# Four buffers for layer 0's normalised rows, and a fourth stage in the expert tiles of a two-layer kernel

## What is computed

```python
    x = L0_attn_u
    xn = _layernorm(x, axis=-1)
    x = x + _L0_attn_ref(xn, ...) + _L0_ffn_ref(xn, ...)
    xn = _layernorm(x, axis=-1)
    x = x + _L1_attn_ref(xn, ...) + _L1_ffn_ref(xn, ...)
```

## Time and profile before

| what | value |
|---|---|
| median of three runs | 1592.26 us |
| the profiled execution's own time | 1595.26 us |
| its span, first to last instruction | 1593.5 us |
| PE busy | 1453.8 us (91%) |
| DVE, ACT, POOL busy | 839.1, 526.5, 578.4 us |
| mean granted TensorE clock | 0.954 of full |
| chain that ended last | PE 86%, DVE 5%, issue 4%, DMA 2%, ACT 1% |

### The profile page before, as it was taken

How to read it: one execution, slowest core, us unless ns; L and a number is a source line. 1 busy time by engine, 2 the same in 40 slices (tenths; PEclk the granted TensorE clock), 3 DMA queues, 4 the chain that set the end, 5 groups by cost and what they waited for, 6 DMA issues and landing times.

```text
span 1593.5 us, 29535 instructions
## 1 busy us (share of the span) xinstructions
PE 1453.8 (91%) x10753; PEld 1151.7 (72%) x10753; DVE 839.1 (53%) x2307; ACT 526.5 (33%) x1099; POOL 578.4 (36%) x762
## 2 busy tenths in 40 slices
PE   7996999999999998999997899999998979997866
PEld 6886789999999997666665566666665647776744
DVE  4554444444444443788875666666666534333414
ACT  2221122222222222333332545454444434433300
POOL 2444421111111111222224455646563454455460
PEclk9998999999999999999997999999999989999987
DMA  5893811111111114100002111111100004434431
GB/s 177 149 104 44 99 48 50 52 47 48 48 50 51 47 48 122 38 0 0 0 0 64 31 31 32 28 34 27 36 21 15 2 18 129 134 119 133 120 123 62
DMA packets 73185, 94.77 MB, mean 59 GB/s; under 512 B 14877, under 2 KB 61367, under 8 KB 73056
## 3 DMA queue, kind: packets, MB, share of 16 engines
q1 hardware_dynamic: 55440, 56.54, 15.6%
q0 software_dynamic: 17616, 36.48, 8.3%
HBM read 60.66 MB, written 32.31 MB: 58 GB/s over the span
## 4 chain that ended last, share of the span: by engine, by line
PE 86%; DVE 5%; issue 4%; DMA 2%; ACT 1%; another core or an unknown queue 1%; POOL 0%; DVEq 0%; ACTq 0%; POOLq 0%
PE score L1591 49%; PE mixed L1591 18%; PE side L1591 13%; DVE WGU L1458 2%; PE side L1793 2%; DMA xn_rows<-XN 2%; PE side L1600 1%; PE mixed L1960 1%; PE side L1953 1%; PE side L1739 0%; PE side L1858 0%; DVE stats L1027 0%; DVE X L1483 0%; DVE X L1558 0%
## 5 line engine op out<-in xcount | busy, mean ns | idle before, releaser
L707 POOL DMA_INDIRECT XN<-xn_rows,slot_tok x149 | 141.4, 949 | 399.5 <-PE side L1793 365.3
L1458 DVE TENSOR_REDUCE WGU<-score 128x2 f32<-128x256 f32 (+1 forms) x256 | 130.8, 553 | 153.3 <-PE score L1591 151.2
L1591 PE MATMUL score<-xT,HT 128*128 128x128 f32 x1136 | 208.0, 275 | 0.0
L743 POOL TENSOR_SCALAR_AFFINE_SELECT ARENA<-ARENA 128x256 f32<-128x256 f32 x256 | 104.2, 431 | 185.1 <-ACT ARENA L944 184.0
L1591 PEld LDWEIGHTS score<-xT,HT 128*128 128x128 f32 x1136 | 166.8, 192 | 0.0
L944 ACT ACTIVATE ARENA<-score 128x768 f32<-128x768 f32 x128 | 103.8, 811 | 148.3 <-PE score L1591 145.9
L1257 DVE TENSOR_TENSOR HT<-sh_gu,score 128x128 f32<-128x128 f32 (+1 forms) x149 | 71.3, 478 | 148.7 <-ACT sh_gu L909 71.3
L657 POOL DMA_INDIRECT lists<-token_no,w_in x128 | 125.4, 980 | 44.2 <-issue 32.3
L1591 PE MATMUL score<-ARENA 32*128 32x256 f32 (+1 forms) x2048 | 126.8, 353 | 12.0 <-DVE WGU L1458 6.0
L1591 PE MATMUL mixed<-ARENA,HT 128*128 x568 | 134.2, 379 | 0.0
L909 ACT ACTIVATE sh_gu<-score 128x128 f32<-128x128 f32 (+1 forms) x149 | 64.1, 430 | 191.3 <-PE score L1591 172.8
(11 more groups left out here) (249 smaller groups left out, 2714.8 us busy)
## 6 DMA issues: line engine op xcount, KB each, us to landing
y_rows<-sh_gu SPq DMA_DIRECT2D x149, 128.0 KB
xn_rows<-XN SPq DMA_DIRECT2D x32, 256.0 KB
WGU<-in_gu SPq DMA_DIRECT2D x8, 1024.0 KB
X<-in_u SPq DMA_DIRECT2D x16, 256.0 KB
ARENA<-in_dn SPq DMA_DIRECT2D x8, 512.0 KB
out<-X SPq DMA_DIRECT2D x16, 256.0 KB
XN<-xn_rows,slot_tok POOLq DMA_INDIRECT x149
lists<-token_no,w_in POOLq DMA_INDIRECT x128
```

The source lines that it names most:

```text
L707: x["got"][j % RING].mark(eng.indirect_dma_start(XG[j % RING], None, xn_rows[l], bass.IndirectOffsetOnAxis(slot_tok[:, j:j + 1], 0)))
L743: ins = eng.affine_select(out=m, in_=m, compare_op=ALU.is_ge, fill=0.0, base=0, pattern=[[0, 2], [1, P]], channel_multiplier=-1)
L1458: ins = eng.tensor_reduce(o, score[:, 2 * h:2 * h + 2, c * P:(2 * c + 1) * P], AX.X, ALU.max, negate=True)
L1591: return eng.matmul(o, l, r, start=start, stop=stop)
```

## The change

Three things are done.

The normalised rows of layer 0 get four buffers, `XN0`: the two of `XN` and two in the region of `ARENA` that later holds the last expert's down weights. Sequence n uses buffer n % 4, and `norm_apply` waits for the store of sequence n-4. The wait for PE's transposes of sequence n-2 stays. The load of the last expert's down weights waits for the last transposes and for the last stores from the two new buffers.

The expert tiles of both layers get a stage `ahead` between `new` and `r`. Tile t is gathered, transposed and copied in turn t, its weights are copied in turn t+1 (`ahead`), its gate and up products come in turn t+2, its down product in turn t+3. There is one turn more. On PE `down` now comes ahead of `xt`, and on ACT `y_copy` ahead of `xt_copy`.

`UPS` has seven sequences in place of eight, seven turns apart from turn 46 on rather than six; nine come after the tiles. `finals` moves the early `finish` calls two turns back.

The diff, cut to its core (the other places pass the buffers on: the waits ahead of layer 0's gathers on POOL, and the operands of the transposes):

```diff
@@ -34,7 +34,7 @@
-UPS = {20: 0, 40: 1, 46: 2, 52: 3, 58: 4, 64: 5, 70: 6, 76: 7}
+UPS = {20: 0, 40: 1, 46: 2, 53: 3, 60: 4, 67: 5, 74: 6}
@@ -144,18 +144,19 @@
-    return [[tile(t - k, count) for k in range(3)] for t in range(count + 2)]
+    return [[tile(t - k, count) for k in range(4)] for t in range(count + 3)]
...
-    end = N1 + 2
+    end = N1 + 3
+    finals = {FINALS_AT + 5 + 4 * n: n for n in range(EARLY)}
     for t in range(end + NSEQ - EARLY + 2):
...
-        last = (t - FINALS_AT - 3) // 4 if t < end and (t - FINALS_AT - 3) % 4 == 0 else EARLY + t - end - 2 if t > end + 1 else None
-        yield t, [tile(t - k) for k in range(3)], *(None if n is None else of(n) for n in (up, down, last))
+        last = finals.get(t) if t < end else EARLY + t - end - 2 if t > end + 1 else None
+        yield t, [tile(t - k) for k in range(4)], *(None if n is None else of(n) for n in (up, down, last))
@@ -260,6 +261,8 @@
     XN = [sb(f"XN{u}", [P, CH, D]) for u in range(2)]
+    last_dn = ARENA[:, (E - 1) * I0 // P * D:].rearrange("p (u c d) -> p u c d", u=2, c=CH)
+    XN0 = [t[:, :, :] for t in XN] + [last_dn[:, u, :, :] for u in range(2)]
@@ -381,7 +384,7 @@
-        n["stored"] = [ev(f"norm_stored{u}", 1, 16, "sync", b // 2) for u in range(2)]
+        n["stored"] = [ev(f"norm_stored{u}", 1, 16, "sync", b // len(XN0)) for u in range(len(XN0) if l == 0 else 2)]
@@ -551,10 +554,15 @@
             N[0]["xn"].wait(eng, n)
-            N[0]["stored"][n % 2].mark(eng.dma_start(rows0[:, n * CH:(n + 1) * CH, :], XN[n % 2][:, :, :]))
+            v = n % len(XN0)
+            N[0]["stored"][v].mark(eng.dma_start(rows0[:, n * CH:(n + 1) * CH, :], XN0[v]))
...
         for e in range(E):
+            if e == E - 1:
+                N[0]["tr"].wait(eng, NSEQ - 1)
+                for v in (2, 3):
+                    N[0]["stored"][v].wait(eng, NSEQ // len(XN0) - 1)
@@ -913,13 +921,13 @@
-            def body(new, r, old):
+            def body(new, ahead, r, old):
                 if r:
                     silu(r)
+                if old:
+                    y_copy(old)
                 if new:
                     xt_copy(new)
-                if old:
-                    y_copy(old)
@@ -1036,10 +1044,15 @@
-            ne["stored"][r.u].wait(eng, r.half, 1)
+            if l == 0:
+                rows, turn = XN0[r.n % len(XN0)], r.n // len(XN0)
+                ne["stored"][r.n % len(XN0)].wait(eng, turn, 1)
+            else:
+                rows = XN[r.u]
+                ne["stored"][r.u].wait(eng, r.half, 1)
@@ -1256,15 +1269,15 @@
-            def body(new, r, old):
-                if new and l == 1:
-                    both_weights(new)
-                if new and l == 0 and new.n:
-                    gate_weights(new)
+            def body(new, ahead, r, old):
+                if ahead and l == 1:
+                    both_weights(ahead)
+                if ahead and l == 0 and ahead.n:
+                    gate_weights(ahead)
                 if r:
                     h_stage(r)
-                if new and l == 0 and new.n:
-                    up_weights(new)
+                if ahead and l == 0 and ahead.n:
+                    up_weights(ahead)
@@ -1823,15 +1837,15 @@
-            def body(new, r, old):
+            def body(new, ahead, r, old):
                 if r:
                     gate(r)
                     if l == 0:
                         up(r)
+                if old:
+                    down(old)
                 if new:
                     xt(new)
-                if old:
-                    down(old)
```

9 lines of the change are left out of this document (5 added, 4 removed).

## The result

The changed kernel takes 1581.45 us, median of four runs (1577.64 to 1582.5), against 1592.12 for the kernel before on the same occasion (1591.78 to 1592.51): ratio 0.9929, interval 0.9911 to 0.9946. It is 10.7 us faster. I had forecast 22.8 us less and 1569.5 us, so the sign was right, the size less than half, and the time inside the range (1556 to 1584) near its slow end.

What follows compares the result with a forecast made beforehand. PE bounds layer 0's tiles, with slack at the front, in layer 1's tiles and behind them. Terms -8.0 - 13.0 - 7.0 + 5.2 = -22.8 us give 1572.5, less 3.0 for the median: 1569.5 us, range 1556 to 1584.

Steps and rivals of the forecast that it cites:

- Four row buffers: Front: DVE's and PE's waits for a late store of normalised rows go, less some given back; -8.0 us.
- I take back 2.7 us: Front: part of the 10.7 us gain returned, about a quarter of ACT's 9.86 us wait after eight scatters.
- Layer 0's tiles: The extra stage there gains nothing, since PE has no idle time and does the same products reordered; 0 us.
- Turns 1 to 46: Layer 1's tiles: PE's wait for ACT's copy goes, 42 turns save 0.31 us each; -13.0 us.
- From turn 46: Layer 1's later tiles: one shared sequence leaves (5.2 us) and 1.8 us of PE's waits go; -7.0 us.
- Behind the tiles: After the last tile: the ninth shared sequence comes on top; +5.2 us, with ends 0 and +9.
- Rival 1: Second half of layer 1's tiles: POOL's unseen stops double, +5.6 there, 1582 us in all; 14 in 100.
- Rival 2: Second half of layer 1's tiles: PE never holds POOL up again, -19 there, 1557.5 us; 15 in 100.
- Rival 3: Front gives nothing, because the scatters' landing sets the lists and the gain is waited for again; 1577.5 us; 10 in 100.
- Rival 4: Layer 1's tiles: POOL's DMAs stretch by one 0.44 us weight copy per turn; 1589.4 us; 3 in 100.
- Rival 5: ACT's 30.6 us stop comes inside layer 1's tiles, with PE behind it; 1600 us; 5 in 100.
- standstill: Behind the tiles: ACT stands still 30.59 us while POOL issues 32 indirect DMAs; used as fact, cause unknown.

Runs made afterwards that it cites:

- paced_burst: Changed kernel with POOL's last 32 gathers in groups of four, each waiting until the previous sequence is added: 1562.36 us, ratio 0.9793 to the kernel before.
- front_only: Kernel before with nothing but the four row buffers: 1589.63 us, ratio 0.9975 to the kernel before.
- after_again: Changed kernel unaltered, run once more: 1583.67 us, ratio 0.9914 to the kernel before.
- two_buffers: Changed kernel with two row buffers in place of four: 1590.51 us, ratio 0.9973 to the kernel before.
- eight_shared: Changed kernel with the eight shared sequences of before put back between its tiles: 1571.28 us, ratio 0.9873 to the kernel before.
- all_four_again: Changed kernel with eight shared sequences, paced last gathers, three later gate/up loads, two down loads behind the list; repeat, kernel before at 1533 us: 1512.7 us, 0.9845.
- after_third: Changed kernel unaltered, run later when the kernel before took 1533 us: 1513.79 us, ratio 0.9878 to the kernel before.

## Why the prediction was right in sign and wrong in size

**Four row buffers, -8.0.** Measured -5.6 at the first gather and -5.3 where layer 1's tiles begin. The mechanism held: the 10.98 us became 1.93. The step that failed is "I take back 2.7 us": 10.9 us were won at the third doubled turn and 5.6 were left, so 5.3 went back, 4.3 of them to the starved products from 179.40 to 193.70. I had booked the return to ACT's wait and looked for the end of the front in the scatters; it lies on PE, behind whose products the list is transposed. The other failure is silent in this pair of profiles. "Waits for the store of four sequences earlier, landed long before" is not true in general: stores took up to 49.9 us from issue to landing (paced_burst's chain of waits), and three of the profiles with four buffers have two waits for one: front_only 3.8 and 3.7, after_again 4.6 and 5.6, paced_burst 7.1 and 7.8. The means of the first gather, 227.3 and 216.9, say the part is worth some 10 us. By the times it is 4 (front_only) or 7 to 9 (two_buffers' 0.9973 against 0.9914 and 0.9929), with wide intervals. I can't narrow that down.

**Layer 0's tiles, 0.** Right: from the first gather to layer 1's tiles both kernels took 1090.2 and 1090.5 us.

**Turns 1 to 46, -13.0.** Measured -10.2 here, and 84.1 to 86.4 us in all profiles with the deep tiles against 95.2 to 96.9 without. The 1.54 us per turn is right. What I left out is small: one more transpose turn to fill the pipeline (1.1 us) and gaps of 0.48, 0.45, 0.49 and 0.67 us, the last three about the turns at which DVE works on the third list.

**From turn 46, -7.0.** Measured -2.9 in this pair, and -0.3 between the means of three profiles without the change (106.8, 108.1, 106.5) and four with it (106.8). This is the step that failed most. I had booked PE's whole sequence of 5.2 us as a gain of this stretch, though I wrote that "PE is not the only limit". While the engines are starved between the gathers, taking work from PE gains little: eight_shared and the kernels built on it put the sequence back for 0.7 to 2.0 us. In the later condition, without starvation, the stretch went from 89.1 to 87.1 by depth (all_four_again) and to 84.4 without the sequence: 2.0 and 2.7, 4.7 in all, where I had 1.8 and 5.2.

**Behind the tiles, +5.2.** Measured +4.8; +6.2 by eight_shared. Right.

**The sum.** In the profiles it came to -13.6 where I had -22.8. Of the 9.2 us that are missing the front has 2.7, turns 1 to 46 2.8 and the stretch from turn 46 4.1, and behind the tiles 0.4 come back. The other 2.9 us are the profiled execution: I took 3.0 us off for the median of the kernel before and let this pass as if it were the same in both, but the changed kernel's profiled execution stood only 0.2 above its own median. So -13.6 came out as -10.7. There is a slip in the prediction, too: its best ends, -11.5, -13.5, -19 and 0, add up to -44 (1548) and not to -38 (1554). The forecast does not use it.

**The rivals.** Rival 1 has the right place and direction: POOL's waits without a releaser in the stretch went from 10.8 to 13.6 us, more but not double. Rival 2 came half way and brought nothing: POOL's waits for PE from turn 46 on went from 14.3 to 6.8 us, and the stretch gained 2.9. Only in the later condition did PE nearly stop holding POOL up (2.3 us, 8.8 without the change), and there the stretch gained 4.7 us, not 19; PE is busy for 79.5 of its 84.4 us. Rival 3 fell, a part of the front's gain arrived, and it was not the landing of the scatters that ended the front. Rival 4 fell: with a turn every 1.54 us the 45 gathers of the tiles up to turn 46 have a mean of 951 ns, against 949 before, and the 29 from turn 46 on 961, against 966, beside 32 weight copies on DVE of 445 ns. In the changed kernel's trace of both stretches the 19 gathers that overlap a copy by more than 0.2 us have a mean of 980 ns, the 31 that overlap none 944. The rule of the Trainium skill, page "SBUF — State Buffer", section "Who interferes with whom", would have stretched them by the length of a copy if these copies run in a two-port mode, which the profile does not show; in this trace they are 0.04 us longer in the mean. Rival 5 fell, no long standstill came inside the tiles.

What my chances lacked was the view that the "standstill" which I used as a fixed fact (30 us of ACT) stood for a loss larger than every term of the sum. One row of waits to be explained was worth more than the change: 21 us for two lines.

## What to carry to other kernels

Where an engine's waits are not of its own making, work of that engine is worth little as a saving: one shared sequence of 5.2 us cost 0.7 to 2.0 us inside such a stretch, and its full length where it stood alone. A wait booked to "issue" or "remote" while one engine sends indirect transfers in an unbroken row is to be tested by pauses, before anything else is tuned around it. And a front whose waits hang on the landing of transfers varies by up to 10 us between profiles: two of them don't size a change there, the same kernel has to be profiled again. Which of two waits that end close together sets the time is seen by whether the engine behind them stood idle: the list was there 6 us before PE turned to it, so bringing it earlier gained nothing.

## What was not expected of the hardware

- An unbroken row of 32 indirect DMAs on POOL, 1.25 us each, left PE with one product every 0.7 to 2.8 us for some 25 us, from about the fourteenth of the row to 4 us past the last. Plain transfers of the same bytes from SP did not. With two pauses of some 3 us the gaps of PE behind the tiles fell to one of 1.07 us. In the later condition the same row left none (stretch of 54.1 us in after_third, 83.8 in the first).
- The granted clock follows: 0.79 of full in the mean of the stretch with the starved products. The eight at 1545.53, after 25 us of single products, took 3.78 us where 1.89 is usual, with a granted clock of 0.50 there: the lower level, 1.2 and not 2.4 GHz. In the same stretch of after_third, with PE busy, it was 0.96.
- The same kernel took 1592 to 1595 us on three chips and later 1533 on three, one of them the same. Of the 55.7 us between two profiles of it 46.3 lie where POOL sends indirect DMAs in pairs or in an unbroken row, 2.5 before the first gather and some 9 in layer 1's front with its scatters; tiles with one gather each did not change. The cause is not known.
- The stores of 256 KB that a DVE wait hung on took 30 to 50 us from issue to landing (30.49 before, 33.04 in two_buffers, 43.63, 45.67 and 49.92 in front_only, after_again and paced_burst) while loads of 1 MB and the scatters filled the transfer engines (DMA share 0.98 from 45 to 110 us of the kernel before).
